# Half of the weighting of one-hot pieces goes from the vector engine to GpSimd, in the stage that turns expert slots into tokens

## The reference, cut to what matters

```python
T = xf.shape[0]                        # 32 images x 257 rows = 8224 tokens
cap = int(CAP_FACTOR * T / E)          # 321
probs = jax.nn.softmax(h @ r2_w.T, -1)
topp, topi = jax.lax.top_k(probs, TOPK)          # two experts a token
...
score = jnp.where(routed, probs, -jnp.inf)
idx = jnp.argsort(-score, axis=0)[:cap].T        # token of each slot of each expert
valid = jnp.take_along_axis(routed.T, idx, 1)
...
xe = xf[idx]                                     # gathered rows
...
ye = jnp.einsum('eci,eoj->eco', ...)
out = jnp.zeros((T, C), xf.dtype).at[idx.reshape(-1)].add((w[..., None] * ye).reshape(-1, C))
```

## Time and profile before

| | |
|---|---|
| time, median of 3 | 1470.26 us (1467.83 to 1470.56) |
| the profiled execution's own time | 1475.44 us |
| its span in the trace | 1473.3 us |
| mean granted PE clock | 0.922 of full |
| busy: PE, DVE, ACT, POOL | 88%, 82%, 61%, 32% of the span |

### The profile page before, as it was taken

How to read it: one execution, slowest core, us unless ns; L and a number is a source line. 1 busy time by engine, 2 the same in 40 slices (tenths; PEclk the granted TensorE clock), 3 DMA queues, 4 the chain that set the end, 5 groups by cost and what they waited for, 6 DMA issues and landing times. The chain is left out here.

```text
span 1473.3 us, 33346 instructions
## 1 busy us (share of the span) xinstructions
PE 1289.9 (88%) x11964; PEld 1047.0 (71%) x11964; DVE 1215.4 (82%) x3143; ACT 893.2 (61%) x1604; POOL 474.8 (32%) x451
## 2 busy tenths in 40 slices
PE   3799999999999999999986233389999999999996
PEld 2457666666766766666766232389999999999996
DVE  4589999999999999999868878867777777777773
ACT  1377887878878888887761252445555555455552
POOL 0122233233233233233211000144454555554543
PEclk8699999999999999999975555689999999999999
DMA  7534345445445435432040500056556565565652
GB/s 231 143 93 131 111 115 132 113 112 136 116 106 137 121 106 135 122 100 61 27 136 16 92 0 1 6 175 173 148 174 179 147 199 156 153 199 150 171 148 24
DMA packets 128186, 176.71 MB, mean 120 GB/s; under 512 B 19946, under 2 KB 116476, under 8 KB 123964
## 3 DMA queue, kind: packets, MB, share of 16 engines
q1 hardware_dynamic: 110652, 153.80, 34.7%
q0 software_dynamic: 17408, 21.25, 8.7%
HBM read 133.85 MB, written 41.15 MB: 119 GB/s over the span
## 5 line engine op out<-in xcount | busy, mean ns | idle before, releaser
L857 ACT ACTIVATE at<-ps_s 128x1024 f32<-128x1024 f32 x256 | 248.4, 1027 | 6.4 <-PE ps_s L670 5.3
L2220 POOL DMA_INDIRECT out_rows<-ye,slot_token x96 | 151.3, 1576 | 229.5 <-ACT ye L2065 216.6
L247 PE MATMUL ps_s<-xet,whi 128*128 128x322 f32 x640 | 205.5, 321 | 12.9 <-issue 11.4
L249 PE MATMUL ps_s<-xet,whi 128*128 128x322 f32 x640 | 199.0, 311 | 0.0
L248 PE MATMUL ps_s<-xet,wlo 128*128 128x322 f32 x640 | 198.4, 310 | 0.0
L2034 ACT ACTIVATE sg<-ps_s 128x322 f32<-128x322 f32 x160 | 70.7, 442 | 172.7 <-PE ps_s L249 172.7
L2135 DVE TENSOR_TENSOR wlo<-raw,whi 128x640 fp32r<-128x640 f32 x192 | 154.0, 818 | 2.3 <-ACT whi L2044 1.3
L2118 DVE TENSOR_TENSOR hm<-ps_s,sg 128x322 f32<-128x322 f32 x128 | 63.2, 494 | 100.2 <-ACT sg L2034 98.7
L686 PE MATMUL ps_av<-at,uv 128*16 128x257 f32 x2048 | 136.2, 383 | 1.0 <-ACT at L901 0.5
L247 PEld LDWEIGHTS ps_s<-xet,whi 128*128 128x128 f32 x640 | 121.3, 189 | 20.9 <-issue 20.4
L247 PE MATMUL ps_av<-whi,hs 128*128 128x256 f32 (+1 forms) x480 | 134.5, 280 | 0.8 <-DVE wlo L2135 0.5
(11 more groups left out here) (380 smaller groups left out, 3596.4 us busy)
## 6 DMA issues: line engine op xcount, KB each, us to landing
raw<-in_wexp SPq DMA_DIRECT2D x32, 1280.0 KB, 6.3
halo<-gray_dram SPq DMA_DIRECT2D x96, 288.0 KB
xb<-in_x SPq DMA_DIRECT2D x64, 384.0 KB, 4.7
raw<-in_wexp SPq DMA_DIRECT2D x32, 640.0 KB, 7.9
gray_dram<-g SPq DMA_DIRECT2D x32, 256.0 KB, 3.3
out_rows<-h SPq DMA_DIRECT2D x64, 128.0 KB, 3.1
token_rows<-xf SPq DMA_DIRECT2D x64, 128.0 KB, 2.3
pre_dram<-pre SPq DMA_DIRECT2D x30, 128.0 KB, 1.7
```

What stands on the lines that cost most here:

```text
L247: nc.tensor.matmul(o, lh, rh, start=first, stop=False)
L249: return nc.tensor.matmul(o, lh, rl, start=False, stop=last)
L857: nc.scalar.activation(at[:, t, 2 * i:2 * i + 2, :, 0:R].rearrange("p j k q -> p (j k) q"), ps_s[i][:, :, :, :].rearrange("p j k q -> p (j ...
L2220: nc.gpsimd.indirect_dma_start(out=out, out_offset=bass.IndirectOffsetOnAxis(ap=slot_token[0:w, 3 * m + st:3 * m + st + 1], axis=0), in_=y ...
```

## The change

Three of the six weightings of `hi_pt[k][..., 96:192]` leave DVE's program and stand in POOL's: piece (44, 65) of k = 0 and pieces (22, 44) and (44, 65) of k = 1. POOL waits for `hot_hi` as ACT does, and signals a new semaphore `hot_pool`, for which PE waits ahead of those three pieces, beside `hot_done`.

```diff
+        hot_pool = sem("hot_pool")
+        BY_POOL = ((0, 44), (1, 22), (1, 44))
...
@@ POOL's program of the routing block, behind its memsets
+            for k, q0 in BY_POOL:
+                q1 = NQ if q0 == pieces[2][0] else q0 + 22
+                pool.wait_ge(hot_hi, k + 1)
+                nc.gpsimd.tensor_tensor(by2(hi_pt[k][:, q0:q1, H3:2 * H3]), by2(at_hi[k][:, q0:q1, :]), twos(code2[:, :, :], H3)[:, q0:q1],
+                                        ALU.mult).then_inc(hot_pool, 1)
...
@@ PE's program
                     pe.wait_ge(hot_done, len(pieces) * k + i + 1)
+                    if (k, q0) in BY_POOL:
+                        pe.wait_ge(hot_pool, BY_POOL.index((k, q0)) + 1)
...
@@ DVE's program
                 for q0, q1 in pieces:
-                    nc.vector.tensor_tensor(by2(hi_pt[k][:, q0:q1, H3:2 * H3]), by2(at_hi[k][:, q0:q1, :]), twos(code2[:, :, :], H3)[:, q0:q1], ALU.mult)
+                    if (k, q0) not in BY_POOL:
+                        nc.vector.tensor_tensor(by2(hi_pt[k][:, q0:q1, H3:2 * H3]), by2(at_hi[k][:, q0:q1, :]), twos(code2[:, :, :], H3)[:, q0:q1], ALU.mult)
```

## The result

The changed kernel takes 1479.24 us (median of 6, 1477.23 to 1479.91) against 1469.32 us for the kernel before (median of 6 on the same chips): a ratio of 1.0064, 95% interval 1.0051 to 1.0077. By the ratio that is 9.4 us more, between 7.5 and 11.3. The forecast was 1478.5, +8.2 us.

The account below looks back on a forecast made before the run. DVE's stream in the routing block's last step was taken to set the end. POOL's 12.1 us, less 0.75 hidden and 3.41 removed, plus 0.3 lost overlap, gave +8.2 us: from 1470.26 to 1478.5 us, range 1472 to 1484.

Parts of the forecast that it names:

- What bounds the step: Routing block's last step: DVE's stream sets the end, so a microsecond there is a microsecond of the kernel.
- What is removed: Three weightings leave DVE's stream in the routing block's last step, taking 3.41 us off the path.
- Exclusion: DVE instructions with two SBUF inputs and POOL's reading ones block each other, except 0.25 us for each POOL instruction.
- POOL's price: Three multiplications of 6144 columns on POOL: 12.1 us, between 11.3 by slope and 12.85 in proportion.
- those two rivals: POOL's multiplications at half price, +2.2 us, 1472.5 us, chance 0.10; at twice the price, +20.3 us, 1490.6 us, chance 0.09.
- PE adds its last piece only: End of the routing block's last step: PE's last piece follows DVE at once, at clock 1.00, taking 1.91 us.
- Turn only at a gap: POOL enters only at DVE gaps, two pieces behind DVE's last; PE's slow clock adds 1.4 us: 1479.9 us, chance 0.27.
- taking turns: Main case: POOL and DVE alternate in the routing block's last step, +8.2 us, 1478.5 us, chance 0.44.
- No exclusion: POOL's pieces do not block DVE, so the change gains the removed 3.4 us: 1466.9 us, chance 0.10.

Follow-up runs that it names:

- extra_product: Kernel before, plus POOL making the three products into scratch tiles that nobody reads; ratio 1.0062 against the kernel before.
- pool_last: Changed kernel, but POOL waits until DVE's last one-hot is done; ratio 1.0046 against the kernel before.
- extra_grouped: Kernel before plus POOL's three products into scratch, DVE doing each k's three weightings, then its three low codes; 1480.15 us (kernel before 1471.52).
- late_second_half: Changed kernel, but POOL takes all three pieces of k = 1, released after DVE's last one-hot of k = 0; ratio 1.0044 against the kernel before.
- extra_late: Kernel before plus POOL's three products into scratch, released when three low codes are done; 1475.04 us (kernel before 1471.52).
- act_piece: Kernel before, but ACT instead of DVE weights piece (44, 65) of k = 1; ratio 0.9988 against the kernel before.
- extra_copy: Kernel before, plus POOL copying the three pieces (one input) into scratch tiles that nobody reads; ratio 1.0028 against the kernel before.
- spread_turns: Changed kernel, but POOL's second and third piece wait until two low codes are done; ratio 1.0064 against the kernel before.
- extra_first_early: Kernel before plus POOL's three products into scratch, first released with the high code, others after three low codes; 1481.56 us (kernel before 1472.38).
- extra_at_two: Kernel before plus POOL's three products into scratch, released when two low codes are done; 1483.12 us (kernel before 1472.38).
- one_piece: Changed kernel, but POOL takes only piece (44, 65) of k = 1; ratio 1.0011 against the kernel before.

## Why the prediction was right, point by point

**What bounds the step** was right: the end of the experts' wait moved by 8.42 us with 8.38 us of the step. **What is removed**, 3.41 us, was right: extra_product, where nothing is removed, has DVE's end 3.39 us later than the changed kernel.

**Exclusion** was right, and is shown, not only argued: 0 for a POOL that writes, 4.94 us for copies with one input, 10.12 us for products with two, with DVE's and PE's programs the same in all three.

**POOL's price** was mis-sized. I took 12.1 us less 0.75 for the hidden heads, 11.35 us, plus 0.3 us of lost overlap between DVE's rows: 11.65 us. Measured are 10.12 us for both. Undisturbed the pieces take 10.76 us in pool_last, 3.56 us for 2016 columns. The end that went by the slope between 512 and 544 columns (11.3 us) was nearer than that in proportion (12.85 us), which spreads the fixed cost of a short instruction over every column. The 4497 ns for 2048 f32 columns of the Trainium skill's GPSIMD Engine Reference (Elementwise, side-by-side cycle accounting), from which the prediction worked an estimated 13.5 us, is further off, for these bf16 operands. bf16 and runs of two made POOL neither much cheaper nor dearer, which settles those two rivals. Where a trace has two sizes of an operation, a slope and a fixed cost can be the better estimate for a size far above both, as they were here.

**PE adds its last piece only** is the step that failed. I held PE's tail at 2.00 us "since the last pieces come at the spacing of before". They don't: two of the last three lost their weighting and come 1.54 us apart, where PE needs 1.87. And PE was not free when they came, since it had taken up k = 0 late and at a granted clock of 0.57. Its last piece ran at 1.00, as I had said, but behind a backlog. The tail is 3.66 us, 0.70 of the 1.66 more from the spacing (extra_grouped) and the rest, as argued above, from the slow start. The two errors, -1.5 and +1.66 us, cancel by luck, and the sum of 8.2 lies near the 8.38 measured for no better reason.

**The rivals.** *Turn only at a gap*: not in the changed kernel, where POOL was let in behind 930.82 and 935.88 in the middle of the stream, but the behaviour exists (late_second_half, extra_late). Its time was not measured with exactly these places, one piece at the gap and two at the end. pool_last and late_second_half, where all three come behind DVE, are 0.87 and 0.98 us below taking turns, not 1.4 us above: in pool_last PE's clock was up again before its last piece. *No exclusion*: excluded. Its 3.4 us were too much in any case, as far as can be argued from act_piece, where PE's tail took back 0.35 us of the 1.13 us removed near the end.

## What to carry to other kernels

Before giving a busy vector engine's work to idle GpSimd, look in the trace for one vector instruction with two SBUF inputs that starts while GpSimd reads, and compare its duration with its undisturbed form; if it waits, the work moved costs its full price on GpSimd (here 1.65 ns a column) against the price saved (here 0.55), and idle time on GpSimd is worth nothing as long as such vector instructions fill the stretch. ACT, slower for the same piece (4.2 us against 3.56), was the better place: no vector row grew beside it, and PE did not wait for it. And when the producer of a piecewise hand-over is made faster near its end, take the consumer's time for a piece into the sum: here 0.35 to 1.66 us came back there. Measure up to the first instruction that everything waits for, not only to the last one of the work in question: extra_late hides 7.10 us otherwise.

## What the runs showed of the hardware that was not expected

- GpSimd's writes alone, two memsets of 2112 and 2016 bf16 columns in 3.58 us beside DVE's two-input products, left every DVE row at its length.
- POOL's request can be passed over by a stream of overlapping DVE instructions until it drains (4.5 us in late_second_half, 7.9 us in extra_late, there past five instructions that began after it), while in 16 other places (2 each in the changed kernel, extra_product, extra_copy, spread_turns, extra_grouped and extra_first_early, 3 in extra_at_two, 1 in one_piece) it was let in at the next boundary of such a stream.
- PE's granted clock was still at 1.00 in the 2.50 us of idleness of the changed kernel and at 0.57 in the 3 us behind it; after 5.46 us of idleness in spread_turns it was at 0.50 for 29 matmuls. The same 65 matmuls took 8.26 us there and 5.52 in extra_grouped.
